# A fused attention and feed-forward kernel: where the block sums of a weight matrix are formed

## The chip, the cores and the metric

The kernel runs on one core of a Trainium2 chip. The metric is device time in microseconds (us) of one execution; the kernel before took 1820.25 us (median of 3 runs, 1819.62 to 1823.83). A core has five engines with instruction queues of their own: PE (TensorE, the matmuls; PEld is its weight load), DVE (VectorE), ACT (ScalarE), POOL (GpSimd) and SP (SyncE, which here only issues DMAs). They meet through semaphores. Sixteen DMA engines move data.

## The reference

Eight batches of 224 tokens of width 512 attend to 750 context rows each (8 heads of 64), and then every token passes through all eight experts of a feed-forward layer:

```
x = x + tanh(g_xattn) * (softmax(q k^T / 8) v @ Wo + bo),  q = layernorm(x) @ Wq, k = ctx @ Wk, v = ctx @ Wv
h = gelu(layernorm(x) @ w1[e] + b1[e])          e = 0..7, 512 -> 1024
y = sum over e of (h @ w2[e] + b2[e])           1024 -> 512
x = x + tanh(g_ffn) * y * norm_gate(x)
```

All inputs are float32. The kernel reaches that precision by splitting each operand into a rounded high part and a low part and adding three products.

## The kernel before

**Stages.** A head, then the attention of batch 0, of batches 1 to 6 (a hardware loop) and of batch 7, then 64 feed-forward steps: two halves of the tokens (896 each), 8 experts, 4 steps of 256 hidden units each. In the attention the order of work on PE, ACT, DVE and POOL is written out in tables (BODY_PLAN, END_PLAN): a word such as `M3.1` is one item of work, `<` means an item of the batch before and `>` one of the batch after. Each engine works its own row off in order; SP's order is the code of its block. PSUM has a ring of four banks, and an item that takes a bank waits until DVE has emptied the bank's last item.

**Items that matter here.** S are scores, R the reciprocal of the softmax row sum, M the scaling of a tile of probabilities (POOL scales the tile of the second query half, L1391), T their transposes on PE (L706), P the product with the values, D the sum of a pair of heads (the split attT, on POOL for odd heads, L1400 and L1402), C the split of the context (L1430, L1433), L and A the layer norms, H the seven products of the very first feed-forward step, which are interleaved into batch 7, W and G the preparation of weights and inputs for them.

**The feed-forward step.** `h = x @ w1` is formed by a scheme with seven block products in place of eight (P1 to P7 in `product`, L754). Its weights are the blocks L11, L12, L21, L22 of the step's part of w1 and sums of them. For each step SP loads four blocks (512 KB, `load_w1`, L497) into `w1_stage`. POOL forms four further blocks from them in `w1_part` (L1487, L1488, L1495, L1501) and splits seven blocks into high and low parts (L1493, L1498 for three, L1504, L1507 for four); then the w2 block (L1518, L1521). It may start to write the split weights of a step once the products of two steps before are done, and the next load of w1 waits for the splits. DVE adds the seven products to the four blocks of h (`h_sums`, L1051), ACT applies gelu, and `second` multiplies with w2 (L781) one step later.

**SP in a middle batch** loads the context of the next batch, stores and reloads x, stores yT, and loads the next batch's rows `xa` (L456) for the layer norm whose first instruction on DVE is L886. In batch 7 it loads the inputs of the feed-forward stage and the first w1 blocks (`load_first`).

Of the kernel before, what the change touches and what calls it, by code (L numbers as in the profile page):

```python
# [5 lines left out]
ALU = mybir.AluOpType  # L6
# [5 lines left out]
P = 128  # L12
# [22 lines left out]
GATE_STEPS = 16  # L35
X_MIXED = ["P7", "P5", "P6", "P4"]
# [51 lines left out]
def plan(text):  # L88

    items = []  # L90
    for word in text.split():
# [22 lines left out]

BODY_PLAN = {
# [22 lines left out]
        D<7 M1.1 L<1.0 L<1.1 M2.1 D1 M3.1 C>0.0 C>0.1 L>0.0 L>0.1 M4.1 D3 M5.1 C>1.0 C>1.1 M6.1 D5 M7.1 M>0.1  # L138
# [25 lines left out]
        D<7 M1.1 L<1.0 L<1.1 Z F M2.1 D1 M3.1 W0.0 G0 G1 G2 W0.1 W0.2 D3 W0.3 G3 W0.4 D5 W1.0 D7 W1.1 W1.2 W1.3  # L164
# [41 lines left out]
def flamingo_kernel(nc, x, ctx, g_xattn, g_ffn, Wq, Wk, Wv, Wo, bo, gate_w, gate_b, rms_w, w1, b1, w2, b2, out,  # L206
                    x2_scratch, xt_scratch):
# [11 lines left out]
    with ExitStack() as st:  # L219
# [117 lines left out]
        b1_loaded, b2_loaded = sem("b1_loaded"), sem("b2_loaded")  # L337
        small_loaded, small_set = sem("small_loaded"), sem("small_set")
# [96 lines left out]
        def _(sp):  # L435
# [43 lines left out]

            load_w(0)  # L480
# [45 lines left out]
            def load_first():  # L526
# [5 lines left out]
                sp.wait_ge(in_psum["S"], number(("S", 0, G - 1, 1), B - 1))  # L532
                load_w1((0, 0, 0))
                sp.dma_start(b1T[:, :], b1).then_inc(b1_loaded, 16)

            def batch(name, plan, b):
# [25 lines left out]
                if name != "last":  # L562
                    load_ctx(b + 1, 1)

# [54 lines left out]
        def _(pe):  # L619
# [16 lines left out]
            def make(item, b, bank_table):  # L636
                kind = item[0]
                if kind in "RMDLAWGUZCNF":
                    return
# [233 lines left out]
        def _(dve):  # L873
# [160 lines left out]
            def h_sums(g, name):  # L1034

                product, other, q, after = {"U2": ("P6", 4, 3, None), "C11": ("P2", 4, 0, None),
                                            "U3": ("P7", 3, 2, None), "C22": ("P5", 2, 1, "U3"),
                                            "V": ("P5", 3, 3, "U3"), "C21": ("P4", 2, 2, "C22"),
                                            "C12": ("P3", 3, 3, "V")}[name]
# [9 lines left out]
                if name == "U2":  # L1049
                    dve.wait_ge(p1_out, upto(1, g, 1))  # L1050
                dve.tensor_tensor(h_sum[:, q, :], product_bank(g, product)[:, 0:TH], h_sum[:, other, :],  # L1051
                                  ALU.add).then_inc(sum_out, 1)
# [317 lines left out]
        def _(pool):  # L1370
# [13 lines left out]
            def handle(item, b):  # L1384
# [8 lines left out]
                elif kind == "D" and item[2] % 2:  # L1393
# [10 lines left out]
                    if pair == 1:  # L1404
                        bias_x(b)
                elif kind == "G":
# [44 lines left out]

            def bias_x(b):
# [22 lines left out]
            def w1_part(g, k):  # L1475
# [4 lines left out]
                def after(n):  # L1480
                    pool.wait_ge(w1_step, upto(6, g, n))
                    alone(pool, passed["pool"])

                if k == 0:
                    pool.wait_ge(w1_loaded, upto(16, g, 16))
                    alone(pool, passed["pool"])
                    pool.tensor_tensor(raw[:, 4], raw[:, 0], raw[:, 3], ALU.add).then_inc(w1_step, 1)  # L1487
                    pool.tensor_tensor(raw[:, 6], raw[:, 1], raw[:, 0], ALU.subtract).then_inc(w1_step, 1)  # L1488
                elif k == 1:
                    if not early(g, 2):  # L1490
                        pool.wait_ge(mix_psum, upto(NM, g, -NM))
                        alone(pool, passed["pool"])
                    pool.tensor_copy(w[:, 0, 0:3], raw[:, 1:4]).then_inc(w1_step, 1)  # L1493
                    after(1)
                    pool.tensor_tensor(raw[:, 5], raw[:, 4], raw[:, 1], ALU.subtract).then_inc(w1_step, 1)  # L1495
                elif k == 2:
                    after(3)
                    pool.tensor_tensor(w[:, 1, 0:3], raw[:, 1:4], w[:, 0, 0:3].bitcast(F32),  # L1498
                                       ALU.subtract).then_inc(w1_split, 1)
                    after(4)  # L1500
                    pool.tensor_tensor(raw[:, 7], raw[:, 2], raw[:, 5], ALU.subtract).then_inc(w1_step, 1)  # L1501
                elif k == 3:
                    after(5)
# [108 lines left out]
```

## Time and profile before

| | |
|---|---|
| median of 3 runs | 1820.25 us |
| profiled execution: span from first to last instruction | 1816.1 us |
| what the median holds beyond that span | 4.15 us |
| PE busy | 1794.9 us, 99% of the span |
| DVE, POOL, ACT busy | 1330.5, 1184.1, 810.9 us |
| granted TensorE clock, mean of the span | 1.000 of full speed |
| DMA traffic | 110.35 MB, 61 GB/s |

The profiled execution has a span and no time of its own apart from it; so the sums are made against the span, and the 4.15 us are taken to stay. Busy time counts neither waits nor DMA issues. "Idle before" in a row is the idle time of that engine just before the instruction, and the name behind the arrow is what ended it. Where an engine is busy all the time and another one is not, only what delays the busy one shows in the end.

### The profile page before, as it was taken

What the parts mean: (1) busy time and instruction counts of PE and PEld (TensorE: products, weight loads), DVE (VectorE), ACT (ScalarE), POOL (GpSimd) and SP (SyncE); (2) the same over time, 40 slices, a digit from 0 to 9 for tenths busy, and PEclk for the clock granted to TensorE, in tenths of its full rate; (3) what the DMA queues carried; (4) which work ended last, traced back from release to release, by engine and by line L of the source; (5) the groups of instructions that cost most, each with busy time, mean ns of one, the idle gap of its engine ahead of it and who ended that gap; (6) DMA issues with size and microseconds to landing.
All of it is one profiled execution on the core that took longest, in us unless ns stands there. A gap on an engine that the chain in (4) does not pass through costs nothing.

```text
span 1816.1 us, 31801 instructions
## 1 busy us (share of the span) xinstructions
PE 1794.9 (99%) x9720; PEld 1615.8 (89%) x9720; DVE 1330.5 (73%) x2308; ACT 810.9 (45%) x1574; POOL 1184.1 (65%) x900
## 2 busy tenths in 40 slices
PE   7999999999999999999999999999999999999999
PEld 7999999999999878888888888888888888888887
DVE  7888878888888877666666766588766767676657
ACT  6767677677766832323232323243232323232322
POOL 5525445263544679777777777699877777777743
PEclk9999999999999999999999999999999999999999
DMA  5111202021120222111111111123412121212111
GB/s 176 39 41 36 57 22 61 21 62 40 34 69 16 92 97 74 66 54 62 58 58 58 58 58 58 47 66 106 127 57 63 52 69 47 69 46 69 46 47 53
DMA packets 52057, 110.35 MB, mean 61 GB/s; under 512 B 13208, under 2 KB 25496, under 8 KB 52000
## 3 DMA queue, kind: packets, MB, share of 16 engines
q1 hardware_dynamic: 52000, 109.64, 19.3%
q8 instruction: 30, 0.49, 0.1%
q14 instruction: 27, 0.22, 0.0%
HBM read 98.61 MB, written 11.01 MB: 60 GB/s over the span
## 4 chain that ended last, share of the span: by engine, by line
PE 96%; DVE 1%; issue 1%; ACT 1%; DMA 0%; SPq 0%; POOL 0%; ACTq 0%; DVEq 0%
PE bank L781 33%; PE scores L754 28%; PE bank L625 19%; PE scores L696 5%; PE bank L706 4%; PE bank L718 4%; PE bank L632 1%; PE scores L839 0%; DVE h_sum L1051 0%; DMA ctx_raw<-in_ctx 0%; ACT hs L1318 0%; PE bank L754 0%; ACT probs L1190 0%; DVE xs L900 0%; ACT h_full L1317 0%
## 5 line engine op out<-in xcount | busy, mean ns | idle before, releaser
L781 PE MATMUL bank<-w2s,hs 128*128 128x512 f32 x2688 | 620.9, 389 | 1.3 <-DVE xres L1018 1.0
L781 PEld LDWEIGHTS bank<-w2s,hs 128*128 128x128 f32 x2688 | 504.4, 188 | 105.1 <-issue 1.5
L754 PE MATMUL scores<-xs,w1s 128*128 128x448 f32 x2646 | 549.5, 366 | 3.6 <-DVE h_sum L1051 3.5
L754 PEld LDWEIGHTS scores<-xs,w1s 128*128 128x128 f32 x2646 | 495.8, 188 | 48.7 <-DVE h_sum L1051 3.8
L1051 DVE TENSOR_TENSOR h_sum<-scores,h_sum 128x448 f32<-128x448 f32 x441 | 262.7, 619 | 183.3 <-PE scores L754 182.8
L1317 ACT ACTIVATE h_full<-h_sum,b1T 128x448 f32<-128x448 f32 x256 | 170.9, 668 | 303.1 <-DVE h_sum L1051 292.4
L1066 DVE TENSOR_TENSOR acc<-bank,acc 128x512 f32<-128x512 f32 x337 | 229.1, 686 | 71.5 <-PE bank L781 62.9
L900 DVE TENSOR_TENSOR hs<-h_full,hs 128x448 fp32r<-128x448 f32 x256 | 237.9, 930 | 52.2 <-ACT hs L1318 52.1
L1190 ACT ACTIVATE h_sum<-scores 128x448 f32<-128x448 f32 x63 | 34.3, 545 | 475.4 <-PE scores L754 475.4
L1391 POOL TENSOR_SCALAR probs<-probs,row_inv 112x750 f32<-112x750 f32 x60 | 130.6, 2176 | 100.1 <-DVE row_inv L989 100.1
L1493 POOL CAST w1s<-w_stage 128x768 fp32r<-128x768 f32 x64 | 69.0, 1078 | 168.5 <-PE scores L754 168.5
L1318 ACT ACTIVATE hs<-h_sum,b1T 128x448 fp32r<-128x448 f32 x256 | 167.7, 655 | 0.0
L1521 POOL TENSOR_TENSOR w2s<-w_stage,w2s 128x1024 fp32r<-128x1024 f32 x64 | 155.1, 2423 | 11.5 <-POOL w2s L1518 11.5
L1507 POOL TENSOR_TENSOR w1s<-w_stage,w1s 128x1024 fp32r<-128x1024 f32 x64 | 155.0, 2422 | 11.3 <-POOL w1s L1504 11.3
L625 PE MATMUL bank<-ctxT,wk 128*128 128x376 f32 (+1 forms) x768 | 147.0, 341 | 8.0 <-DVE ctxT L900 8.0
L625 PE MATMUL bank<-wv,ctxT 128*125 128x256 f32 x1152 | 152.1, 283 | 0.0
L625 PEld LDWEIGHTS bank<-wv,ctxT 128*125 128x125 f32 x1152 | 142.6, 186 | 1.0
L625 PEld LDWEIGHTS bank<-ctxT,wk 128*128 128x128 f32 x768 | 131.5, 191 | 10.4 <-issue 9.4
L1498 POOL TENSOR_TENSOR w1s<-w_stage,w1s 128x768 fp32r<-128x768 f32 x64 | 137.8, 2153 | 0.0
L1234 ACT ACTIVATE probs<-scores,neg_max 112x750 f32<-112x750 f32 x128 | 113.3, 886 | 32.1 <-DVE neg_max L983 20.8
L900 DVE TENSOR_TENSOR probsT<-bank,probsT 125x448 fp32r<-125x448 f32 x192 | 115.9, 618 | 12.7 <-ACT probsT L1190 11.1
L1190 ACT ACTIVATE probsT<-bank 125x448 fp32r<-125x448 f32 x192 | 100.0, 542 | 49.3 <-PE bank L706 49.0
(128 smaller groups left out, 2197.3 us busy)
## 6 DMA issues: line engine op xcount, KB each, us to landing
w_stage<-in_L_ffn_w SPq DMA_DIRECT2D x128, 512.0 KB, 3.5
ctx_raw<-in_ctx SPq DMA_DIRECT2D x16, 376.0 KB, 3.2
ctx_raw<-in_ctx SPq DMA_DIRECT2D x14, 374.0 KB, 3.2
xa<-in_x SPq DMA_DIRECT2D x16, 224.0 KB, 2.7
xres<-in_x SPq DMA_DIRECT2D x16, 224.0 KB, 2.7
x_scratch<-xres SPq DMA_DIRECT2D x16, 224.0 KB, 2.3
xt_scratch<-yT SPq DMA_DIRECT2D x16, 224.0 KB, 2.8
x_raw<-xt_scratch SPq DMA_DIRECT2D x4, 896.0 KB, 7.7
```

The source lines that it names most:

```text
L625: mm = pe.matmul(bank, s[i], m[j], start=first and n == 0, stop=last and n == total - 1)
L754: mm = pe.matmul(product_bank(g, name)[:, 0:TH], w1s[j % 2][:, s, W_OF[name], kc, :], xs[:, i, m, kc, :], start=n == 0, stop=n == 5)
L781: mm = pe.matmul(bank[:, :], hs[j % 2][:, s, ht, t * P:(t + 1) * P], w2s[j % 2][:, m, ht, :], start=n == 0, stop=n == 5)
L900: return dve.tensor_tensor(out, a_, b_.bitcast(F32), ALU.subtract)
L1051: dve.tensor_tensor(h_sum[:, q, :], product_bank(g, product)[:, 0:TH], h_sum[:, other, :], ALU.add).then_inc(sum_out, 1)
L1066: dve.tensor_tensor(home, ps[(3 * j + t) % RING][:, :], b2_sum[:, :] if first else home, ALU.add).then_inc(y_added, 1)
L1190: return act.activation(dst, src, ACT.Copy, scale=scale)
L1317: act.activation(h_full[:, q, :], src, ACT.Gelu, bias=bias)
L1318: act.activation(hs[j % 2][:, 0, ht, half * TH:(half + 1) * TH], src, ACT.Gelu, bias=bias).then_inc(h_act, 1)
L1498: pool.tensor_tensor(w[:, 1, 0:3], raw[:, 1:4], w[:, 0, 0:3].bitcast(F32), ALU.subtract).then_inc(w1_split, 1)
L1507: pool.tensor_tensor(w[:, 1, 3:7], raw[:, 4:8], w[:, 0, 3:7].bitcast(F32), ALU.subtract).then_inc(w1_split, 1)
L1521: pool.tensor_tensor(w[:, 1], w2_stage[:, :, :], w[:, 0].bitcast(F32), ALU.subtract).then_inc(w2_split, 1)
```

## The change

The four sums per step are no longer formed by POOL in the feed-forward stage. The w1 input is laid out anew in DRAM (one array per block, padded to 7 units of 80 rows of 2048 floats). During the attention, seven times:

- SP copies four blocks of one unit from the input to a DRAM scratch `w1_sums` (`copy_blocks`, at the end of batches 0 to 6), 655,360 bytes each.
- One batch later POOL issues seven accumulating DMAs (destination += source, DRAM to DRAM, 655,360 bytes each) in three phases, items `E<0`, `E<1`, `E<2`: four DMAs, then two, then one. Phase 0 waits for the copies, phase 1 for the four DMAs of phase 0, phase 2 for the two of phase 1.

The sums in scratch have the sign that an accumulation gives, so some products come out negative; `h_sums` subtracts where it added before. A step's load is now two DMAs of rows of 1 KB: three blocks from the input and four from scratch, 896 KB instead of 512 KB. In batch 7 SP waits for all 49 accumulating DMAs before the first of these loads.

```diff
 BODY_PLAN pool:
-        D<7 M1.1 L<1.0 L<1.1 M2.1 D1 M3.1 C>0.0 C>0.1 L>0.0 L>0.1 M4.1 D3 M5.1 ...
+        D<7 E<0 M1.1 L<1.0 L<1.1 M2.1 E<1 D1 M3.1 C>0.0 C>0.1 L>0.0 L>0.1 E<2 M4.1 D3 M5.1 ...
 END_PLAN pool:
-        D<7 M1.1 L<1.0 L<1.1 Z F M2.1 D1 M3.1 W0.0 G0 G1 G2 W0.1 W0.2 D3 ...
+        D<7 E<0 M1.1 L<1.0 L<1.1 Z F E<1 M2.1 D1 M3.1 E<2 W0.0 G0 G1 G2 W0.1 W0.2 D3 ...
+            def copy_blocks(u):
+                for k, block in enumerate(("L22", "L11", "L11", "L12")):
+                    sp.dma_start(unit_of(w1_sums, k, u), unit_of(w1, W1_BLOCKS.index(block), u)
+                                 ).then_inc(blocks_copied, 16)
 load_w1:
-                sp.dma_start(w1_stage[:, 0:4], w1[e, j]).then_inc(w1_loaded, 16)
+                sp.dma_start(w1_stage[:, 0:3], step_of(w1, 1, 4, e, j)).then_inc(w1_loaded, 16)
+                sp.dma_start(w1_stage[:, 3:7], step_of(w1_sums, 0, 4, e, j)).then_inc(w1_loaded, 16)
 load_first:
+                sp.wait_ge(blocks_added, 112 * UNITS)
                 load_w1((0, 0, 0))
 SP, end of batches 0 to 6:
                     load_ctx(b + 1, 1)
+                    copy_blocks(b)
 h_sums:
+                if op == "less product":
+                    dve.tensor_tensor(h_sum[:, q, :], kept, new, ALU.subtract).then_inc(sum_out, 1)
+                else:
+                    dve.tensor_tensor(h_sum[:, q, :], new, kept,
+                                      ALU.add if op == "sum" else ALU.subtract).then_inc(sum_out, 1)
+            def add_blocks(u, phase):
+                if phase == 0:
+                    pool.wait_ge(blocks_copied, u * 64 + 64)
+                    terms = [(k, "L21") for k in range(4)]
+                elif phase == 1:
+                    pool.wait_ge(blocks_added, u * 112 + 64)
+                    terms = [(1, "L22"), (3, "L22")]
+                else:
+                    pool.wait_ge(blocks_added, u * 112 + 96)
+                    terms = [(3, "L11")]
+                alone(pool, passed["pool"])
+                for k, block in terms:
+                    pool.dma_start(unit_of(w1_sums, k, u), unit_of(w1, W1_BLOCKS.index(block), u),
+                                   accum_op=ALU.add, max_dma_last_dim=8192).then_inc(blocks_added, 16)
 w1_part (the four tensor_tensor of raw[:, 4] to raw[:, 7] go; what is left):
+                    pool.tensor_copy(w[:, 0, 0:3], raw[:, 0:3]).then_inc(w1_step, 1)
+                    pool.tensor_tensor(w[:, 1, 0:3], raw[:, 0:3], w[:, 0, 0:3].bitcast(F32),
+                                       ALU.subtract).then_inc(w1_split, 1)
+                    pool.tensor_copy(w[:, 0, 3:7], raw[:, 3:7]).then_inc(w1_step, 1)
+                    pool.tensor_tensor(w[:, 1, 3:7], raw[:, 3:7], w[:, 0, 3:7].bitcast(F32),
+                                       ALU.subtract).then_inc(w1_split, 1)
```

POOL in a middle batch, before, from the scaling M1.1 (first row) over the layer norm's two small instructions to M2.1 and the split attT of the pair D1:

```order
L1391 TENSOR_SCALAR probs<-probs,row_inv 112x750 [waits inv_out]
L1380 REGISTER_ALU
L1381 TENSOR_TENSOR rstd<-rstd,minus_half 112x1 [waits ln_var]
L1380 REGISTER_ALU
L1381 TENSOR_TENSOR rstd<-rstd,minus_half 112x1 [waits ln_var]
L1389 REGISTER_ALU
L1391 TENSOR_SCALAR probs<-probs,row_inv 112x750 [waits inv_out]
L1396 ISA
L1398 REGISTER_ALU [waits P_lo_out]
L1400 CAST attT<-att_sum 128x224 [waits O_in_psum]
```

The same place after the change (the scaling is now L1424, attT L1433; w_sums is the scratch, and the first row is one of four alike):

```order
L1500 DMA w_sums<-in_L_ffn_w 80x2048
L1422 ISA
L1424 TENSOR_SCALAR probs<-probs,row_inv 112x750 [waits inv_out]
L1413 REGISTER_ALU
L1414 TENSOR_TENSOR rstd<-rstd,minus_half 112x1 [waits ln_var]
L1413 REGISTER_ALU
L1414 TENSOR_TENSOR rstd<-rstd,minus_half 112x1 [waits ln_var]
L1422 REGISTER_ALU
L1424 TENSOR_SCALAR probs<-probs,row_inv 112x750 [waits inv_out]
L1493 ISA
L1500 DMA w_sums<-in_L_ffn_w 80x2048 [waits blocks_added]
L1500 DMA w_sums<-in_L_ffn_w 80x2048
```

Four DMAs now stand ahead of M1.1, and behind M2.1 a wait for the four with two more DMAs ahead of D1.

POOL in batch 7, before, from M3.1 (first row) through the first weight blocks:

```order
L1391 TENSOR_SCALAR probs<-probs,row_inv 112x750 [waits inv_out]
L1487 TENSOR_TENSOR w_stage<-w_stage 128x256 [waits w1_loaded]
L1488 TENSOR_TENSOR w_stage<-w_stage 128x256
L1473 TENSOR_TENSOR x_mix<-x_raw 128x896 [waits S_in_psum,x_raw_loaded]
L1473 TENSOR_TENSOR x_raw<-x_raw 128x2x448 [waits x_mixed,S_in_psum,x_raw_loaded]
L1473 TENSOR_TENSOR x_mix<-x_raw 128x896 [waits x_mixed,S_in_psum,x_raw_loaded]
L1493 CAST w1s<-w_stage 128x768 [waits P_in_psum]
L1495 TENSOR_TENSOR w_stage<-w_stage 128x256 [waits w1_step]
L1498 TENSOR_TENSOR w1s<-w_stage,w1s 128x768 [waits w1_step]
L1501 TENSOR_TENSOR w_stage<-w_stage 128x256 [waits w1_step]
```

The same place after the change:

```order
L1424 TENSOR_SCALAR probs<-probs,row_inv 112x750 [waits inv_out]
L1500 DMA w_sums<-in_L_ffn_w 80x2048 [waits blocks_added]
L1524 TENSOR_TENSOR x_mix<-x_raw 128x896 [waits S_in_psum,x_raw_loaded]
L1524 TENSOR_TENSOR x_raw<-x_raw 128x2x448 [waits x_mixed,S_in_psum,x_raw_loaded]
L1524 TENSOR_TENSOR x_mix<-x_raw 128x896 [waits x_mixed,S_in_psum,x_raw_loaded]
L1536 CAST w1s<-w_stage 128x768 [waits P_in_psum,w1_loaded]
L1540 TENSOR_TENSOR w1s<-w_stage,w1s 128x768 [waits w1_step]
```

The four sums are gone, the last accumulating DMA stands ahead of the inputs' sums, and the wait for the loaded weights has moved to the first rounding.

SP in batch 7 after the change, at the first loads of the feed-forward stage (x_raw are its inputs, w_stage the weights, h_full here takes b2):

```order
L533 DMA x_raw<-xt_scratch 128x2x896
L520 DMA w_stage<-in_L_ffn_w 128x3x256 [waits blocks_added,S_in_psum]
L521 DMA w_stage<-w_sums 128x4x256
L559 DMA b1T<-in_L_ffn_b 128x64
L486 DMA xt_scratch<-yT 512x1x112 [waits Y_lo_out]
```

Before there was one w_stage load here, and it waited for S_in_psum alone.

## Rows read from the trace of the kernel before

**Rows 1.** The page, part 1: busy time, share of span, instructions.

```profile
PE 1794.9 (99%) x9720; PEld 1615.8 (89%) x9720; DVE 1330.5 (73%) x2308; ACT 810.9 (45%) x1574; POOL 1184.1 (65%) x900
```

**Rows 2.** Stretches: length, then busy time of each engine, clock, DMA share, GB/s.

```profile
256.00:334.00 78.00, 77.94 (x539) 74.89 (x538) 64.02 (x137) 54.69 (x121) 36.28 (x30) 1.00 0.16 43
567.00:650.00 83.00, 78.86 (x480) 69.89 (x479) 70.45 (x137) 62.19 (x122) 49.77 (x41) 1.00 0.19 62
...
1260.00:1800.00 540.00, 540.00 (x2519) 471.47 (x2518) 368.01 (x558) 164.37 (x274) 387.76 (x286) 1.00 0.20 63
```

**Rows 3.** PE's waits, whole run: us in total, times, longest.

```profile
PE bank L625 <- DVE ctxT L900: 8.0, 1, 8.0
PE scores L754 <- DVE h_sum L1051: 3.5, 6, 0.9
```

**Rows 4.** The chain that ended last, two feed-forward pieces: start, us, what.

```profile
1283.52 9.54 PE bank L781 x42
1293.05 8.51 PE scores L754 x42
```

**Rows 5.** Instructions on tile w_stage: count, ns min/median/max.

```profile
L1501 POOL TENSOR_TENSOR w_stage<-w_stage x64: 731/1120/1592, 617.2 to 1775.9; 128x256 f32<-128x256 f32 x64
```

**Rows 6.** POOL in one feed-forward step: start, us, instruction [idle before].

```profile
1283.69 0.83 POOL L1493 CAST w1s<-w_stage 128x768 fp32r<-128x768 f32 x1 [2.33 <-PE scores L754]
...
1290.59 2.40 POOL L1507 TENSOR_TENSOR w1s<-w_stage,w1s 128x1024 fp32r<-128x1024 f32 x1 [0.18 <-POOL w1s L1504]
```

**Rows 7.** The page, part 3: DMA queue, packets, MB, share of 16 engines' span.

```profile
q1 hardware_dynamic: 52000, 109.64, 19.3%
```

**Rows 8.** The page, part 6: DMA issues, count, KB each, us to landing.

```profile
w_stage<-in_L_ffn_w SPq DMA_DIRECT2D x128, 512.0 KB, 3.5
...
xa<-in_x SPq DMA_DIRECT2D x16, 224.0 KB, 2.7
```

**Rows 9.** POOL in the middle batch from 263 us: M1.1, M2.1, D1, M3.1, M4.1.

```profile
265.06 2.17 POOL L1391 TENSOR_SCALAR probs<-probs,row_inv 112x750 f32<-112x750 f32 x1
...
284.57 2.17 POOL L1391 TENSOR_SCALAR probs<-probs,row_inv 112x750 f32<-112x750 f32 x1
289.05 0.37 POOL L1400 CAST attT<-att_sum 128x224 fp32r<-128x224 f32 x1 [2.30 <-DVE att_sum L1010]
...
291.42 2.17 POOL L1391 TENSOR_SCALAR probs<-probs,row_inv 112x750 f32<-112x750 f32 x1 [1.25 <-DVE row_inv L989]
...
302.32 2.18 POOL L1391 TENSOR_SCALAR probs<-probs,row_inv 112x750 f32<-112x750 f32 x1
```

**Rows 10.** PE in the same batch: the transposes T1 and T3.

```profile
273.43 1.02 PE L706 MATMUL bank<-ident,probs 112*125 112x112 f32 x8
...
297.50 0.59 PE L706 MATMUL bank<-ident,probs 112*125 112x112 f32 x4
```

**Rows 11.** SP in the same batch: the load of the next rows xa.

```profile
287.68 0.33 SPq L456 DMA_DIRECT2D xa<-in_x  x1
```

**Rows 12.** DVE in the same batch: a layer norm applied, and the next one's statistics.

```profile
284.77 0.96 DVE L896 TENSOR_SCALAR xa<-xres,mean_var,rstd 112x512 f32<-112x512 f32 x1
...
293.93 0.69 DVE L886 BATCH_NORM_STATS2 stats<-xa 112x6 f32<-112x512 f32 x1
```

**Rows 13.** POOL in batch 7: end of the pair D<7, M2.1, M3.1, first rounding of w1.

```profile
575.96 0.67 POOL L1402 TENSOR_TENSOR attT<-att_sum,attT 128x224 fp32r<-128x224 f32 x1
...
593.59 2.29 POOL L1391 TENSOR_SCALAR probs<-probs,row_inv 112x750 f32<-112x750 f32 x1 [1.95 <-DVE row_inv L989]
...
601.75 2.17 POOL L1391 TENSOR_SCALAR probs<-probs,row_inv 112x750 f32<-112x750 f32 x1 [0.99 <-DVE row_inv L989]
...
613.94 0.83 POOL L1493 CAST w1s<-w_stage 128x768 fp32r<-128x768 f32 x1
```

**Rows 14.** PE in batch 7: the transposes T2, and the first product H0.

```profile
598.17 1.02 PE L706 MATMUL bank<-ident,probs 112*125 112x112 f32 x8
...
628.95 1.45 PE L754 MATMUL bank<-xs,w1s 128*128 128x448 f32 x6 [0.40 <-DVE b_sum L944]
```

More of the change, by code:

```diff
@@ L35 @@
 GATE_STEPS = 16
+UNITS = B - 1
+UNIT = 5
+UNIT_ROWS = UNIT * P * 2 * P // 2048
 X_MIXED = ["P7", "P5", "P6", "P4"]
@@ L112, with unit_of, step_of @@
 }
+W1_BLOCKS = ("L21", "L11", "L12", "L22")
+def unit_of(t, k, u):
+    return t[k, bass.ds(u * UNIT_ROWS, UNIT_ROWS), :]
+def step_of(t, k0, k1, e, j):
+    rows = P * 2 * P // 2048
+    at = t[k0:k1, bass.ds(e * (JS * rows) + j * rows, rows), :]
+    return at.rearrange("k r (p n) -> (r p) k n", n=2 * P)
 BODY_PLAN = {
@@ L1034, in h_sums @@
             def h_sums(g, name):
[L1036 to L1039, printed above, removed]
+                product, other, q, after, op = {"U2": ("P6", 4, 3, None, "product less"),
+                                                "C11": ("P2", 4, 0, None, "sum"),
+                                                "U3": ("P7", 3, 2, None, "less product"),
+                                                "C22": ("P5", 2, 1, "U3", "sum"),
+                                                "V": ("P5", 3, 3, "U3", "sum"),
+                                                "C21": ("P4", 2, 2, "C22", "sum"),
+                                                "C12": ("P3", 3, 3, "V", "product less")}[name]
                 dve.wait_ge(mix_psum, upto(NM, g, MIX.index(product) + 1))
@@ L1050, in h_sums @@
                     dve.wait_ge(p1_out, upto(1, g, 1))
-                dve.tensor_tensor(h_sum[:, q, :], product_bank(g, product)[:, 0:TH], h_sum[:, other, :],
-                                  ALU.add).then_inc(sum_out, 1)
+                new, kept = product_bank(g, product)[:, 0:TH], h_sum[:, other, :]
+                if op == "less product":
[3 more added lines that the diff above has]
+                                      ALU.add if op == "sum" else ALU.subtract).then_inc(sum_out, 1)
             def h_low(g, q):
@@ L1478, in w1_part @@
                 raw, w = w1_stage, w1s[j % 2]
[L1480 to L1489, printed above, removed]
+                if k == 1:
+                    pool.wait_ge(w1_loaded, upto(32, g, 32))
@@ L1490, in w1_part @@
                     if not early(g, 2):
                         pool.wait_ge(mix_psum, upto(NM, g, -NM))
[L1492 to L1495, printed above, removed]
+                    alone(pool, passed["pool"])
+                    pool.tensor_copy(w[:, 0, 0:3], raw[:, 0:3]).then_inc(w1_step, 1)
@@ L1496, in w1_part @@
                 elif k == 2:
-                    after(3)
-                    pool.tensor_tensor(w[:, 1, 0:3], raw[:, 1:4], w[:, 0, 0:3].bitcast(F32),
+                    pool.wait_ge(w1_step, upto(2, g, 1))
+                    alone(pool, passed["pool"])
+                    pool.tensor_tensor(w[:, 1, 0:3], raw[:, 0:3], w[:, 0, 0:3].bitcast(F32),
                                        ALU.subtract).then_inc(w1_split, 1)
-                    after(4)
-                    pool.tensor_tensor(raw[:, 7], raw[:, 2], raw[:, 5], ALU.subtract).then_inc(w1_step, 1)
```

23 lines of the change are left out of this document (13 added, 10 removed).

## The prediction

> **What bounds the kernel now.** I read the busy shares first. PE is busy for 1794.9 us, 99% of the span, every other engine for 73% or less [rows 1]. Then the stretches, because an average can hide a stage with another limit. In a middle batch of the attention PE works 77.94 of 78.00 us, in the second half of the feed-forward stage 540.00 of 540.00, at the full clock; only the passage between the two stages has a gap, 78.86 of 83.00 [rows 2]. Third, what PE waits for: 8.0 us once in the head, for the split context, and 3.5 us in six pieces for `h_sum` [rows 3]; no row names POOL or a weight. Fourth, the chain that ended last: in the feed-forward stage it is 9.54 us of second products and 8.51 us of first products in turn, all PE, 18.05 us a step [rows 4]. So time can be won only in PE's gaps, and is lost wherever something new comes later than PE wants it.
>
> **The change, part by part.** *POOL's sums go.* Four instructions a step, between 0.73 and 1.12 us each [rows 5], in 64 steps: 187 to 287 us of POOL. In the steady steps this is worth nothing: POOL's first rounding of w1 already waits 2.33 us for PE [rows 6], and its result is used more than a whole step later. *The signs* change one operand order and an ALU code of DVE instructions whose number and size stay: 0.
>
> *Loads of a step.* First a rate: the queue moved 109.64 MB in 19.3% of 16 engines' span [rows 7], so while busy it moves 109.64 MB / (0.193 x 1816.1 us) = 313 KB per us. A 512 KB (524 thousand bytes) load lands in 3.5 us [rows 8]; 524/313 = 1.7 of these are data and 1.8 fixed. The xa load (229 thousand bytes in 2 KB rows, 2.7 us [rows 8]) gives 254 KB per us by the same fixed part. The new 917 thousand bytes take 4.7 us by the first rate, and 9.0 at half the second, which is my bound for rows of 1 KB. What hides it: POOL's work from the first rounding to the last split of w1 now takes 1283.69 to 1292.99, 9.3 us [rows 6], less two sums of 1.1 then 7.1; from there to the next rounding, one step of 18.05 after the first, remain 11.0 us. Hidden at either end. Cost 0.
>
> *Copies on SP.* Four issues at 0.33 us [rows 11], behind the batch's last loads. Queued behind them is the next batch's context load, which waits for POOL's split in any case. Their data, 2.6 MB, has most of a batch before POOL asks for it. Cost 0.
>
> *POOL's DMA issues.* The trace has no DMA on POOL. From below: 0.33 us, SP's issue [rows 11]; from above: 2.17 us, POOL's longest instruction here [rows 9]. I take 1.0, nearer to SP's row, since an issue works on no tile. Four stand ahead of M1.1. In the middle batch M1.1 runs 265.06 to 267.23 [rows 9], and PE wants it at 273.43 [rows 10]: 6.2 us of slack against 4.0, so 0; a loss begins at 1.55 us an issue, and at 2.17 it is 2.5 us a batch, 15 in six. Two more stand behind M2.1, which ends at 286.74, ahead of D1 (289.05) and M3.1 (291.42, 2.17 long) [rows 9], which T3 wants at 297.50 [rows 10]. With D1's 1.1 us they may start as late as 294.2, so the wait in phase 1 may last until 292.2. Phase 2 precedes M4.1 (302.32), with still more room.
>
> *How long four accumulating DMAs take.* No such DMA is in the trace. Each has 655 thousand bytes to read twice (the sum and the block) and to write once. If the passes overlap fully, one pass counts: 2.1 us each at 313 KB per us, four in 10.2 us with 1.8 fixed. If all three come one after another: 6.3 each, four in 26.9. I take the two reads, with the write beside them, since loads, one-sided reads, are what the row of the rate mostly holds: 4.2 each, four in 18.6, two in 10.2, one in 6.0. In a middle batch they start near 266 and have landed at 285, before the wait at 286.74: 0. Phase 1's two, from 289 on, land at 299, before 302: 0.
>
> One rule of the Trainium skill speaks for less: page "Collectives: The Full Stack", section "The bandwidth ceiling: the fold count and why AG ≠ RS ≠ AR", says that a reducing transfer runs at about half a copy's rate, because each chunk has two source reads on one ring, and measures 32.35 against 62.28 GB/s on two DMA engines. No run here shows it yet; by that (16 GB/s per engine) an estimate is 2.6 us a DMA and 12 us for four, and the sum would be 0.
>
> *Batch 7 is the tight one.* The pair D<7 ends at 576.63 [rows 13]; the four DMAs are issued from there, start at 577.6 and land at 596.2. Phase 1 stands ahead of M2.1, which ran at 593.59 [rows 13]. Two issues later, at 598.2, M2.1 starts, ends at 600.5, and T2, which PE ran at 598.17 [rows 14], is 2.3 us late. Phase 1's two land at 607.4; M3.1, 2.3 later than its 601.75, is done at 606.2; phase 2 goes out at 608.4 and lands at 614.4. Only then does SP load the first w1 blocks (behind it wait b1, a store of yT and the next loads, all with more room), which land 4.7 to 5.4 us later, near 619.5. Their rounding ran at 613.94 [rows 13], 616.2 with the shift: 3.3 late. Two sums of at least 0.73 and 1.12 us behind it are gone, some 2 us, so H0, at 628.95 before [rows 14], is late by 2.3 and 1.0: 3.3 us.
>
> *A second rule, on starved descriptors.* The row: DVE's only operation here with SBUF on both sides and one tensor read, the layer norm, runs 0.96 us from 284.77 [rows 12], and phase 1's DMAs are issued after 286.74, so it costs 0; on top of one it would cost at most 0.96 us, 7 in seven batches. The Trainium skill, page "SBUF — State Buffer", section "SBUF: two separate sides", says that a DMA issued by GpSimd cannot write its descriptors while VectorE holds the shared port in a two-port mode. By that rule the sum stays as it is, unless the DMAs slide under such an instruction.
>
> **The sum.** 0 in the head, 0 in the middle batches, +3.3 in batch 7, 0 in the feed-forward steps: 1816.1 + 3.3 of span, and with the 4.15 us by which the median exceeds the span, 1823.5 us. That is within 0.3% (5.5 us, about what a measurement can tell from no change), 1814.8 to 1825.7.
>
> **The rivals.**
>
> *Slower: the accumulations become the bound of the attention's end.* One mechanism: POOL's in-order queue waits for DMAs, and the scalings behind it reach PE late. It decides from 16 us for four in batch 7 (593.4 less 577.6, where T2 begins to slip) and from 26 us in a middle batch (292.2). At the upper end, 26.9 us: the four land at 604.5, M2.1 ends at 608.8, PE is 10.6 late; phase 1's two (14.4 us) land at 619.9, phase 2's one (8.1 us) at 629, the load at 634, against 624.5 with the shift, less the 2 us saved: H0 18 late. In the middle batches 0.7 each, 4 in six. Sum +22: 1842 us. For it: the row rates are those of plain loads, and loads in both directions share 16 engines with the DMAs. Against: the DMA share in these stretches is 0.16 to 0.19 [rows 2], so little competes.
>
> *Slower: the issues, or the xa load.* At 2.17 us an issue the loss is 15 us, as above, and in batch 7 some 3 more. Or phase 1's two DMAs, at 287 to 298, share the engines with the xa load, issued at 287.68 [rows 11] and due at 293.93 [rows 12]: it lands at 290.4, 3.5 us early, and if it takes twice as long, still in time; if three times, DVE stops for 1.9 us, and PE for as much, since its four banks are emptied by DVE. That is 11 in six. Time: 1829 to 1841.
>
> *Faster.* If the POOL time that is freed lets DVE and ACT run earlier in the passage, PE could win there: 4.1 us of idle in 567 to 650 [rows 2] and the 3.5 us behind h_sum [rows 3], 7.6 at the very most, 1812.6; the pieces are waits for DVE, not for POOL, so hardly any of it is to be had. More than 5.5 us would need most of it.
>
> *The change does not do what it says*, that is, POOL keeps its 187 us: excluded, since the instructions are gone; but their going being worth nothing is my forecast.
>
> **How the numbers follow.** Forecast, between 0 and +5: chance 0.54. Slow accumulation: 0.25. Slow issues or xa: 0.16. Faster: 0.05, of which 0.04 by over 0.3%. Slower by over 0.3% is nearly all of the two rivals and a little of the forecast's upper end, 0.42; the rest, 0.54, is no change. The range for 8 in 10 goes from 1817, a few us won in the passage, to 1842, the end of the three-pass bound; the forecast's own is 1820 to 1825.5.
>
> **What would show it.** In the changed profile: POOL busy down by about 200 us and PE's 9.54 and 8.51 us pieces unchanged; no PE wait in a middle batch; POOL idle ahead of phase 1 in batch 7 for a DMA on w_sums, and T2 and H0 late by 2 to 4 us; POOL's DMA issues near 1 us. Wrong, if PE works less than 77.9 of 78 us in a middle batch, if it waits there for probs or DVE for xa, if a step in the feed-forward stage waits for its load, or if four accumulations take over 20 us or under 15.

## The result, and the profile after

The changed kernel takes 1881.3 us (median of 4 runs, 1881.06 to 1884.47), the kernel before 1820.2 beside it (4 runs): ratio 1.0337, 95% interval 1.0322 to 1.0352. I had forecast 1823.5 and a range up to 1842; it is slower than even the range. All times here and below are medians; one run of e7 that took 4616.0 us is left out of its median as a slow run.

First the busy shares of the changed kernel, which answer to [rows 1]:

```profile
span 1879.9 us, 31674 instructions
...
PE 1818.1 (97%) x9720; PEld 1637.0 (87%) x9720; DVE 1343.8 (71%) x2308; ACT 812.5 (43%) x1574; POOL 1028.1 (55%) x693
```

The span grew from 1816.1 to 1879.9, by 63.8 us. PE is idle for 61.8 us (1879.9 less 1818.1) where it was idle for 21.2, and the same 9720 matrix instructions are busy for 23.2 us more. So two losses are to be explained, some 41 us of new waits and some 23 us of slower work. The stretches say where (columns as in [rows 2]: length, busy time of PE, PEld, DVE, ACT, POOL, granted clock, DMA share, GB/s):

```profile
100.00:180.00 80.00, 77.38 (x535) 74.09 (x534) 64.59 (x135) 54.08 (x119) 42.44 (x37) 1.00 0.54 134
180.00:260.00 80.00, 68.78 (x443) 65.48 (x443) 52.37 (x114) 44.78 (x99) 37.06 (x33) 0.89 0.53 127
260.00:340.00 80.00, 73.83 (x475) 70.55 (x474) 57.95 (x124) 48.55 (x107) 35.22 (x32) 0.94 0.52 127
...
580.00:660.00 80.00, 70.25 (x454) 67.54 (x455) 55.01 (x117) 46.17 (x102) 42.84 (x38) 0.91 0.46 114
...
1320.00:1860.00 540.00, 540.00 (x2520) 471.61 (x2519) 370.42 (x553) 163.19 (x273) 301.40 (x174) 1.00 0.26 84
```

The loss is in the attention. The feed-forward stage is what it was: 540.00 of 540.00 us of PE at the full clock, with POOL at 301 us instead of 388. In the attention PE loses up to 11 us in 80, the granted clock goes down to 0.89, and the DMA engines are busy for about half of the time instead of 0.16. What PE waits for (us in total, times, longest), against [rows 3]:

```profile
PE bank L732 <- POOL probs L1424: 30.2, 7, 9.5
PE bank L732 <- DVE queries L990: 12.0, 4, 3.3
PE bank L651 <- DVE ctxT L926: 8.5, 2, 8.2
PE scores L780 <- DVE h_sum L1084: 2.5, 2, 1.8
```

Two waits are new, and 30.2 + 12.0 = 42.2 us is about the new idle time. The transposes wait for the scaling of the probabilities on POOL, and for a DVE instruction on the queries.

**The first wait: POOL's queue stands still.** POOL and then PE in the second batch, start, us, instruction, idle before:

```profile
190.54 0.67 POOL L1435 TENSOR_TENSOR attT<-att_sum,attT 128x224 fp32r<-128x224 f32 x1
191.35 2.54 POOL L1500 DMA_DIRECT2D w_sums<-in_L_ffn_w  x3
204.60 0.81 POOL L1500 DMA_DIRECT2D w_sums<-in_L_ffn_w  x1 [10.71 <-issue]
205.18 2.46 POOL L1424 TENSOR_SCALAR probs<-probs,row_inv 112x750 f32<-112x750 f32 x1
```

```profile
207.78 1.99 PE L732 MATMUL bank<-ident,probs 112*125 112x112 f32 x8 [8.04 <-POOL probs L1424]
```

Each issue takes 0.8 to 0.9 us. But between the third and the fourth of E0's DMAs POOL does nothing for 10.71 us, and nothing in the profile is named that it waits for. M1.1 behind it comes late, and PE stands for 8.04 us. The DMA rows for the first and the third of the three tell when they landed (they were issued at 191.35 and near 193):

```profile
w_sums<-in_L_ffn_w POOLq DMA_DIRECT2D x1, 640.0 KB, 6.0
```

```profile
w_sums<-in_L_ffn_w POOLq DMA_DIRECT2D x1, 640.0 KB, 11.6
```

The first is there at 197.4, the third at 204.6: POOL goes on when all that it sent out has landed, not when the first has. Such gaps stand ahead of the 6th, 11th, 16th, 31st, 41st and 46th of the 49 accumulating DMAs (5 to 12 us each), every fifth; at the 21st, 26th and 36th, each the first of its phase, nothing was out. The line's total:

```profile
L1500 POOL DMA_DIRECT2D w_sums<-in_L_ffn_w x49: 806/915/1686, 110.9 to 666.5; - x49
its engine sat idle before it (us, times) until:
  issue: 52.5, 13
```

**The slower work.** The clock around this stop, in stretches of 2 us:

```profile
198.00:200.00 2.00, 1.74 (x10) 1.33 (x8) 1.09 (x2) 1.64 (x4) 0.00 (x0) 1.00 1.00 201
200.00:202.00 2.00, 0.00 (x0) 0.00 (x0) 1.67 (x4) 0.53 (x2) 0.00 (x0) 0.91 0.95 208
202.00:204.00 2.00, 0.00 (x0) 0.00 (x0) 0.00 (x0) 0.00 (x0) 0.00 (x0) 0.50 0.77 190
...
208.00:210.00 2.00, 2.00 (x10) 2.00 (x11) 0.45 (x1) 1.03 (x2) 0.00 (x0) 0.50 1.00 209
210.00:212.00 2.00, 2.00 (x8) 2.00 (x7) 1.75 (x6) 0.76 (x2) 0.57 (x1) 0.53 0.01 0
212.00:214.00 2.00, 2.00 (x15) 2.00 (x15) 0.41 (x1) 0.96 (x2) 0.00 (x0) 1.00 0.00 0
```

PE stops near 199.7; the granted clock goes from 1.00 to 0.50 (from 2.4 to 1.2 GHz) and is still there when PE works again, until about 212. Eight transposes take 1.99 us instead of 1.02 [rows 10]. So this stop cost 8 us of idle time and some 2 of half-speed work behind it.

**The second wait: the xa load.** SP, DVE and PE in the third batch, against [rows 11, 12]:

```profile
312.04 0.34 SPq L473 DMA_DIRECT2D xa<-in_x  x1
```

```profile
322.46 0.69 DVE L912 BATCH_NORM_STATS2 stats<-xa 112x6 f32<-112x512 f32 x1 [4.17 <-DMA xa<-in_x]
```

```profile
325.28 1.18 PE L732 MATMUL bank<-ident,probs 112*125 112x112 f32 x4 [3.33 <-DVE queries L990]
```

Phase 1's two DMAs were issued at 310.96. The xa load, started at 312.04 beside them, lands 10 us later; DVE, whose queue is in order, stops for 4.17 us ahead of its statistics, the queries behind them are late, and PE stands for 3.33. Part 6 of the page (count, KB each, median us to landing), against [rows 8]:

```profile
w_sums<-in_L_ffn_w POOLq DMA_DIRECT2D x49, 640.0 KB, 8.5
...
w_sums<-in_L_ffn_w SPq DMA_DIRECT2D x28, 640.0 KB, 8.0
...
xa<-in_x SPq DMA_DIRECT2D x16, 224.0 KB, 8.3
```

### The profile page after: what moved, and what is told of

Same layout as the page of the kernel before. It is cut to its first block, busy times and chain, and to the rows that moved or that the text cites. A ratio compares the mean times of both kernels' runs of the same rounds, so it can differ in the third digit from the quotient of the medians.

```text
span 1879.9 us, 31674 instructions
## 1 busy us (share of the span) xinstructions
PE 1818.1 (97%) x9720; PEld 1637.0 (87%) x9720; DVE 1343.8 (71%) x2308; ACT 812.5 (43%) x1574; POOL 1028.1 (55%) x693
## 3 DMA queue, kind: packets, MB, share of 16 engines
q0 software_dynamic: 4704, 32.12, 9.2%
## 4 chain that ended last, share of the span: by engine, by line
PE 82%; issue 8%; DVE 3%; DMA 2%; POOL 2%; ACT 1%; SPq 0%; POOLq 0%; DVEq 0%; ACTq 0%
PE bank L807 32%; PE scores L780 28%; PE bank L651 11%; PE bank L732 3%; PE scores L722 3%; PE bank L744 2%; DMA xa<-in_x 2%; POOL probs L1424 1%; DVE neg_max L1009 1%; PE bank L780 1%; DVE queries L990 0%; PE bank L658 0%; PE scores L865 0%; POOL w_sums L1500 0%; DVE stats L912 0%
## 5 line engine op out<-in xcount | busy, mean ns | idle before, releaser
L1084 DVE TENSOR_TENSOR h_sum<-scores,h_sum 128x448 f32<-128x448 f32 x378 | 223.8, 619 | 144.8 <-PE scores L780 144.4
L926 DVE TENSOR_TENSOR hs<-h_full,hs 128x448 fp32r<-128x448 f32 x256 | 252.2, 986 | 52.9 <-ACT hs L1351 52.8
L1099 DVE TENSOR_TENSOR acc<-bank,acc 128x512 f32<-128x512 f32 x337 | 225.0, 683 | 59.3 <-PE bank L807 58.0
L1223 ACT ACTIVATE h_sum<-scores 128x448 f32<-128x448 f32 x63 | 34.3, 545 | 479.3 <-PE scores L780 479.3
L1424 POOL TENSOR_SCALAR probs<-probs,row_inv 112x750 f32<-112x750 f32 x60 | 136.2, 2270 | 90.9 <-DVE row_inv L1015 90.7
L1547 POOL TENSOR_TENSOR w1s<-w_stage,w1s 128x1024 fp32r<-128x1024 f32 x64 | 162.9, 2545 | 11.3 <-POOL w1s L1543 11.2
L651 PE MATMUL bank<-ctxT,wk 128*128 128x376 f32 (+1 forms) x768 | 152.5, 349 | 8.5 <-DVE ctxT L926 8.5
L732 PE MATMUL bank<-ident,probs 112*125 112x112 f32 x768 | 111.0, 286 | 42.5 <-POOL probs L1424 30.2
L732 PEld LDWEIGHTS bank<-ident,probs 112*125 112x125 f32 x768 | 106.4, 201 | 49.8 <-issue 34.3
L651 PEld LDWEIGHTS bank<-ctxT,wk 128*128 128x128 f32 x768 | 136.7, 198 | 11.2 <-issue 9.7
```

Source lines behind the costliest of these rows:

```text
L651: mm = pe.matmul(bank, s[i], m[j], start=first and n == 0, stop=last and n == total - 1)
L732: last = pe.transpose(bank[0:KT, at:at + QT], probs[0:QT, (h % 2) * 2 + qt, kt * KT:(kt + 1) * KT], ident[0:QT, 0:QT])
L926: return dve.tensor_tensor(out, a_, b_.bitcast(F32), ALU.subtract)
L1084: dve.tensor_tensor(h_sum[:, q, :], new, kept, ALU.add if op == "sum" else ALU.subtract).then_inc(sum_out, 1)
L1099: dve.tensor_tensor(home, ps[(3 * j + t) % RING][:, :], b2_sum[:, :] if first else home, ALU.add).then_inc(y_added, 1)
L1424: pool.tensor_scalar(probs[0:QT, i, :], probs[0:QT, i, :], row_inv[0:QT, i:i + 1], None, ALU.mult).then_inc(probs_scaled[qt], 1)
```

## The experiments

Theory 1: the space for POOL's descriptors, the entries by which its DMAs are handed to the DMA engines (1024 bytes in this program, a number that was there before the change), holds five of these DMAs, and when it is used up POOL stands until everything out has landed. Theory 2: the accumulating transfers share the engines with loads that the attention waits for, xa above all. Theory 3, the rival: what is lost beside that lies in POOL's issues, the copies, the new loads or the signs.

**Four times the space (e1).**

```diff
-    nc = ... dynamic_dma_scratch_size=1024)
+    nc = ... dynamic_dma_scratch_size=4096)
```

> The only edit: the space for the descriptors of POOL's DMAs is 4096 bytes a partition instead of 1024. Theory 1 (the space holds five of the 49 accumulating DMAs; before every further group POOL's queue stands until the earlier ones have landed, and the M1.1 or M2.1 behind it comes late): a four times longer space has that stop at about every 21st DMA, so at 2 places at most instead of 9; of POOL's 52.5 us of idle time ahead of the accumulating DMAs under 15 us are left, of TensorE's 30.2 us of waits for probs under 8, and a part of the 23 us of slower clock goes with them: 1832 to 1846 us. Theory 2 (the accumulating DMAs are slow and share the transfer engines with the loads that the attention waits for): nothing changes, 1876 to 1886 us. Theory 3 (POOL's issue itself costs more than thought): nothing changes either, and the 0.9 us an issue stays as it is under every theory.

1860.2 us, ratio 1.0210 (1.0176 to 1.0245). One stop is left, ahead of the 24th DMA, in batch 4; the next counted place, the 47th, is the first of a phase 1, with nothing out.

```profile
360.34 1.71 POOL L1500 DMA_DIRECT2D w_sums<-in_L_ffn_w  x2
370.33 1.67 POOL L1500 DMA_DIRECT2D w_sums<-in_L_ffn_w  x2 [8.28 <-issue]
```

```profile
PE bank L732 <- DVE queries L990: 18.7, 6, 3.8
...
PE bank L732 <- POOL probs L1424: 6.0, 2, 5.7
```

POOL's idle time ahead of the line fell from 52.5 to 10.0 us and PE's wait for probs from 30.2 to 6.0, as Theory 1 said. The time is worse than I expected from it, because the other wait grew, from 12.0 us in four batches to 18.7 in six.

**Twice the space (e2).** The same line with 2048.

> The only edit: 2048 bytes instead of 1024. Theory 1: the stop comes about every 10th or 11th DMA, so at 4 places instead of 9, each as long as before (up to 12 us) if at the wrap POOL waits for everything that is out; then about half of the loss by the stops stays, 1845 to 1865 us. Theory 1b (POOL waits only until the entries that it needs are free): a DMA ten places back has long landed, so there is no stop at all and the time is that of 4096 bytes. Theories 2 and 3: 1876 to 1886 us.

1866.2 us, 1.0244 (1.0209 to 1.0279), just above the 1865 that was expected at most. Gaps stand ahead of the 23rd, 34th and 45th DMA, every 11th; the 12th is the first of a phase 1, with nothing out.

```profile
360.69 0.86 POOL L1500 DMA_DIRECT2D w_sums<-in_L_ffn_w  x1 [0.44 <-issue]
366.94 2.50 POOL L1500 DMA_DIRECT2D w_sums<-in_L_ffn_w  x3 [5.38 <-issue]
```

The DMA ten places back had landed long ago, so Theory 1b (only the entries needed must be free) falls; POOL waits for all that is out. Periods of 5, 11 and 23 in 1024, 2048 and 4096 bytes put a DMA between 171 and 178 bytes. Counted in entries of 16 bytes, a size that no run here shows, that is 11 entries a DMA and no other whole number.

**No additions (e3).**

```diff
                 elif kind == "E":
-                    add_blocks(b - 1, item[2])
+                    pass
```

SP's wait ahead of the first w1 load is then for the copies.

> Left out: the 49 accumulating DMAs, so that the block sums are copies of single blocks. The 28 copies by SP, the feed-forward loads from the new tensor and the signs in the sums of products stay. Theories 1 and 2: everything that is lost is lost by the accumulating DMAs, so 1816 to 1826 us, with TensorE's waits for probs at 0 and its busy time in the feed-forward unchanged. Rival (the copies, the new loads or the signs cost something): over 1830 us.

1819.8 us, 0.9990 (0.9977 to 1.0004). The xa load takes 2.7 us again.

```profile
span 1818.2 us, 31474 instructions
...
PE 1800.0 (99%) x9720; PEld 1621.3 (89%) x9720; DVE 1341.7 (74%) x2308; ACT 811.7 (45%) x1574; POOL 985.3 (54%) x644
```

Copies, loads and signs together cost nothing that can be measured, and the 200 us that POOL no longer works (985 against 1184 [rows 1]) bring nothing. Theory 3 is left with the issues alone. (PE's busy time differs by 5.1 us from that of before at nearly the same span, so the changed kernel's slower work is 18.1 us against this run and 23.2 against before, its new idle time 43.6 or 40.6.)

**Copies in the place of additions (e4).**

```diff
-                                   accum_op=ALU.add, max_dma_last_dim=8192).then_inc(blocks_added, 16)
+                                   max_dma_last_dim=8192).then_inc(blocks_added, 16)
```

> The 49 DMAs of POOL copy a block instead of adding it to what stands in the sums (same place, same bytes written, half the bytes read; the sums are then single blocks), with 1024 bytes for descriptors. Theory 1: if a copying DMA takes as many entries as an accumulating one, the stops come at the same places and are as long as what is out needs to land: 1850 to 1880 us; if it takes half, they come at every 10th or 11th, 1830 to 1850 us. Theory 2 (transfer time alone): POOL has no stops, and what is late is late by the transfers: the landings and the xa loads are about half as long, so about half of the loss, 1845 to 1855 us.

1828.8 us, 1.0042 (1.0027 to 1.0057), a little under both guesses. Gaps stand ahead of the 11th, 31st and 41st DMA, every 10th, which is 6 entries of 64 for one:

```profile
187.70 1.80 POOL L1500 DMA_DIRECT2D w_sums<-in_L_ffn_w  x3
195.92 0.52 POOL L1500 DMA_DIRECT2D w_sums<-in_L_ffn_w  x1 [6.42 <-issue]
```

The queue's packets (4704) and bytes are those of the changed kernel, but they took 5.2% of the engines' time in place of 9.2%, and the xa load lands in 6.5 us, not 8.3: DVE waits 5.0 us for it in all, not 17.9, and PE 0.9 us for queries. 11 entries against 6 would be 5 rows an engine with two sources against 5 with one, and one entry more, if the 80 rows are spread evenly over 16 engines. That is how the Trainium skill describes the reducing transfer (page "Collectives: The Full Stack", section "The bandwidth ceiling: the fold count and why AG ≠ RS ≠ AR"): it emits two read descriptors per chunk where a copy emits one. The runs agree; the even spread and the one entry more are my inference.

**A smaller space that fits the batch (e5).** The same line with 1280: 80 entries, seven DMAs of 11, just what a batch issues.

> The only edit: 1280 bytes for the descriptors, less than a third of the 4096 that left two stops. From the stops of the three sizes before (every 5th, 11th and 23rd DMA) one accumulating DMA takes 11 entries of 16 bytes, so 1280 bytes hold seven, just what one batch issues. Theory 1: the stop then falls ahead of the first of E0, when all earlier DMAs landed some 40 us before, so POOL never stands: under 3 us of idle time ahead of the accumulating DMAs except where they wait for one another, no wait of TensorE for probs, and less than with 4096 bytes: 1845 to 1856 us. Rival (the more space the better, whatever the count): between the times of 1024 and 2048 bytes, 1866 to 1881 us.

1852.0 us, 1.0164 (1.0136 to 1.0192): less space than 4096 bytes and a better time, though the two ratios' intervals overlap a little. One stop was left, ahead of the 27th DMA, where the count has none. It stands between phase 1's two DMAs of batch 4, and that is the one batch in which PE did not wait for queries (15.9 us in the five others).

**Phase 1 behind the xa load (e6, e7).**

```diff
-        D<7 E<0 M1.1 L<1.0 L<1.1 M2.1 E<1 D1 M3.1 C>0.0 C>0.1 L>0.0 L>0.1 E<2 M4.1 D3 M5.1 ...
+        D<7 E<0 M1.1 L<1.0 L<1.1 M2.1 D1 M3.1 E<1 C>0.0 C>0.1 L>0.0 L>0.1 M4.1 D3 E<2 M5.1 ...
```

In e6 with 1024 bytes, in e7 with 1280.

> 1024 bytes as in the changed kernel; in the middle batches E<1 stands behind M3.1 instead of behind M2.1 and E<2 behind D3, so that the two DMAs of the second phase start when the xa loads have landed. Theory 2: DVE's waits for xa (17.9 us) and TensorE's for queries (12.0 us) go, the xa load takes 2.7 to 4 us again; the stops stay: 1855 to 1870 us. Rival 3 (what is lost beside the stops is lost by POOL's issues or by the sums' transfers elsewhere): 1876 to 1886 us.

> Both edits: 1280 bytes, and E<1 and E<2 later. Theories 1 and 2 together hold all of the loss: no wait for probs, none for queries, a granted clock near 1 through the attention, 1818 to 1828 us. Rival 3: what neither explains stays, over 1835 us.

e6: 1866.3 us, 1.0248 (1.0220 to 1.0277); e7: 1826.0 us, 1.0026 (1.0011 to 1.0040). Both times are as expected. In e6 the wait for queries is gone and the stops are not:

```profile
PE bank L732 <- POOL probs L1424: 26.7, 5, 9.8
```

In e7 the wait for queries is gone, and all stops but one, 5.15 us ahead of the 27th DMA, in batch 4 as in e5:

```profile
378.05 0.80 POOL L1500 DMA_DIRECT2D w_sums<-in_L_ffn_w  x1 [5.15 <-issue]
```

```profile
384.18 1.69 PE L651 MATMUL bank<-wv,ctxT 128*125 128x256 f32 x12 [1.97 <-POOL ctxT L1468]
```

PE waits there 2.0 us for the split context and 0.9 for probs. The middle batch from 256 us, with the DMA engines as busy as in the changed kernel (0.55) and POOL issuing as much, is that of [rows 2]:

```profile
256.00:334.00 78.00, 77.92 (x539) 74.83 (x538) 63.97 (x137) 54.67 (x122) 42.42 (x37) 1.00 0.55 136
```

```profile
294.20 1.74 POOL L1500 DMA_DIRECT2D w_sums<-in_L_ffn_w  x2
```

```profile
294.61 0.68 DVE L912 BATCH_NORM_STATS2 stats<-xa 112x6 f32<-112x512 f32 x1
```

Phase 1 now goes out when xa is there. The four times side by side (us):

| space | E<1, E<2 in place | E<1, E<2 later |
|---|---|---|
| 1024 bytes | 1881.3 | 1866.3 |
| 1280 bytes | 1852.0 | 1826.0 |

The space is worth 29 and 40 us, the order 15 and 26. Together they give 11 us more than the sum of the two alone. A part of that is that a stop between phase 1's two DMAs keeps the second one off the xa load: in the changed kernel batches 1 and 6 had such a stop and no wait for queries, the four between had the wait (12.0 us); with 1280 bytes five batches have it (15.9). With the slower clock behind it, that is about half of the 11 us; the rest is not explained. Theory 3 has at most the 6 us that e7 lies above before, and the one stop that is left takes some 3 of them.

**A short last unit (e8).** This is e7 with one more edit: in batch 7 the seventh unit is added over the two parts that hold weights, not over five.

```diff
+    rows = UNIT_ROWS
+    if isinstance(u, int) and u == UNITS - 1:
+        rows = (NE * JS - (UNITS - 1) * UNIT) * (UNIT_ROWS // UNIT)
...
```

> As the run before, and the seventh unit, of whose five parts only two hold weights, is added over these two parts alone (the padding is left out, the result is the same). Shorter phases in the last batch, in which the feed-forward's first load waits for the last addition: 0 to 4 us less than the run before, 1817 to 1826 us. If the last batch isn't held up by the additions, no difference.

1824.1 us, 1.0013 (1.0001 to 1.0024), 1.9 less than e7, with intervals that overlap. With the order mended, all stops gone but the one in batch 4 (5.17 us here), and the last batch shortened, this is the best version with additions, and it does not beat the kernel before.

**Other spaces (e9, e10, e12).** e9 is e8 with 3712 bytes, e10 the changed kernel with 1408, e12 e8 with 1408.

> As e8_short_last, with 3712 bytes: 232 entries, 21 DMAs of 11 entries, so the stop falls at the 22nd and the 43rd, each the first of a batch, with everything before it landed. With 1280 bytes one stop of 5 us before the 27th DMA was left that this count doesn't explain (TensorE waited 2.0 us for ctxT there). Theory 1 with the count alone: no stop at all, 1819 to 1824 us. If that stop has another cause than the space (it comes at the 27th DMA whatever the size), it is there again: 1822 to 1826 us. Neither theory lets it be faster than before by more than a measurement shows, since without any addition the time was that of before.

> The changed kernel's order with 1408 bytes: 88 entries, eight DMAs. Theory 1: stops at the 9th, 17th, 25th (second, third and fourth of the four DMAs of E0) and 41st (second of E1); those at the 33rd and 49th are hidden behind a wait that is there anyway. So more space than 1280 bytes and more stops: 18 to 35 us of idle POOL ahead of the accumulating DMAs (9.0 with 1280), 1860 to 1872 us against 1852. Rival (more space is better): 1845 to 1853 us.

> As e8_short_last (E<1 and E<2 later, short last unit), with 1408 bytes, the size that showed no stop at all in the changed kernel's order. If the stops belong to the size and not to the order: no stop, no wait for probs or ctxT, granted clock 1.00, 1819 to 1823 us, between e3_copies_only and e8. If a stop shows up at another place it costs 5 to 11 us there, 1824 to 1833 us. In neither case less than before by over 0.3%.

e9: 1830.5 us, 1.0055 (1.0042 to 1.0069), above both guesses. My count was wrong: there is a stop ahead of the 39th DMA,

```profile
498.50 2.54 POOL L1503 DMA_DIRECT2D w_sums<-in_L_ffn_w  x3
511.53 0.80 POOL L1503 DMA_DIRECT2D w_sums<-in_L_ffn_w  x1 [10.48 <-issue]
```

and PE waits 7.9 us. e10: 1855.2 us, 1.0183 (1.0163 to 1.0203), where I expected stops at the 9th, 17th, 25th and 41st and there is none; the time lies between my two guesses. It has no wait for probs, and 18.9 us of waits for queries in six batches. e12: 1829.6 us, 1.0038 (1.0024 to 1.0052): no stop in six batches, and two in batch 7, whose DMAs are of another size.

```profile
578.35 0.85 POOL L1503 DMA_DIRECT2D w_sums<-in_L_ffn_w  x1
584.11 0.77 POOL L1503 DMA_DIRECT2D w_sums<-in_L_ffn_w  x1 [4.91 <-issue]
588.57 1.56 POOL L1503 DMA_DIRECT2D w_sums<-in_L_ffn_w  x2 [3.69 <-issue]
```

So 11 entries a DMA predicts the stops for the three powers of two, and not for 1280, 1408 and 3712 bytes. Which rule holds there stays open; the gaps end, here too, with the landing of what was out (in e9 the third DMA, issued near 499.9, lands after 11.6 us, at 511.5), and e10, without a gap, had no wait for probs.

**A stop without any transfer (e11).** e3 with a pause of POOL in the place of E<0:

```diff
+                elif kind == "E" and item[2] == 0:
+                    for k in range(16):
+                        pool.wait_ge(paused, (b - 1) * 16 + (k + 1))
+                        alone(pool, passed["pool"])
+                        pool.memset(pause[:, :], 0.0).then_inc(paused, 1)
```

> As e3_copies_only (no additions, no transfer of POOL's), with 16 MEMSETs of 128x512 that wait for one another at E<0 of each batch, 10 to 13 us in which POOL does nothing for the others. It prices a stop of POOL by itself, without any transfer: M1.1 had 6.2 us to spare, so TensorE waits 4 to 7 us for probs in each of seven batches, 28 to 48 us of idle time. If TensorE's stops bring the slower clock by themselves, its busy time grows as well, by 10 to 27 us, and the granted clock shows 0.9 to 0.98 in the 80 us stretches: 1858 to 1890 us. Rival (the slow clock comes with the accumulating transfers): busy time as in e3 (1800 us), clock 1.00, 1846 to 1866 us.

1870.4 us, 1.0274 (1.0253 to 1.0294), within what Theory 1 gave.

```profile
span 1867.3 us, 31795 instructions
...
PE 1814.8 (97%) x9720; PEld 1636.0 (88%) x9720; DVE 1345.6 (72%) x2308; ACT 810.8 (43%) x1574; POOL 1042.7 (56%) x757
```

```profile
PE bank L734 <- POOL probs L1427: 32.2, 7, 5.2
```

```profile
180.00:260.00 80.00, 75.59 (x505) 72.59 (x505) 60.31 (x129) 51.80 (x115) 42.82 (x44) 0.96 0.24 75
```

A pause is 16 times 0.53 us and 0.15 us of waiting between two, 10.8 in all; less the 6.2 of slack it should delay PE by 4.6. It does: seven waits of 4.6 us, and beside them 14.8 us more of busy time than in e3, at a granted clock of 0.96 with the DMA share at 0.24. So the slower clock comes with PE's stops and not with the transfers; e7, with all the transfers, has 1.00 from 20 to 580 us. A stop of 4.6 us costs about 2 us more behind it.

## Why the prediction was wrong

**The step that failed: POOL's DMA issues.** I bounded an issue between 0.33 and 2.17 us from the durations of instructions. The duration was right: 0.9 us against my 1.0. What I did not see is that an issue can be refused for a time by a resource that stands in the program with its size, 1024 bytes, and that before the change no DMA of POOL used; e1, e2 and e5 change this number alone, and the stops move or go. The price is not spread over the issues but falls on every fifth, as long as the transfers out need, up to 11.6 us: beyond the 6.2 us of slack that I had worked out for M1.1, and that the pause of e11 confirms. In time it is 29 us as the kernel stands, 40 with the other loss mended. The Trainium skill, page "DMA: Bandwidth & Descriptors", section "SWDGE vs HWDGE vs iDMA", tells of the place: descriptors of GpSimd's DMAs are appended to rings in a carved-out part of SBUF, the on-chip memory, and those of SP's are not. SP's copies, with the same bytes, show no such stop: four issues took 2.6 to 3.6 us in every batch, more than the 1.3 I had taken.

**The xa load: seen, priced too low, and left to a rival.** I wrote that it is due 3.5 us after it lands and that three times its time would stop DVE for 1.9 us, 11 us in six batches. It took 3.1 times (8.3 us) and 3.7 times in e1 (10.0), DVE stopped for up to 5.0 us (e2), and moving phase 1 away was worth 15 to 26 us. The mechanism stood in the rival, but the sum had it at 0: I had no row for a load beside large transfers, and twice its time alone, which I took for harmless, was too little. The Trainium skill, page "DMA: Bandwidth & Descriptors", section "Queues, rings and completion order", says that each engine serves its queues in turn, a packet at a time; a load between two large additions then waits for theirs at each turn. A load that takes 3 to 4 times as long fits that; the page gives no such factor, and no run here shows the turns themselves.

**The clock: not in the sum at all.** Every rival took "late by x" as "longer by x". Of the 63.8 us, 18 to 23 are added busy time, most of it work at the lower clock behind the stops, 0.4 us and more for each us of idle time (e11: 14.8 to 34.3, against e3). With it my own rival's 11 us would have been some 16.

**Right.** The additions' speed: four in a row land in 17.4 us (batch 4: the first issued at 373.70, the last near 376.5 with 14.6 us to its landing) where I took 18.6, and the first of three in 6.0, my figure for one; phase 2's one, beside SP's copies, took 11.1, where nothing hung on it. That fits two reads beside a write, as assumed. The estimate of 12 us for four from the Trainium skill's rate (page "Collectives: The Full Stack", section "The bandwidth ceiling: the fold count and why AG ≠ RS ≠ AR") was too short. So the rival of slow accumulation falls for the middle batches, where it needed 26 us. The copies, the loads of a step (the second part, issued 0.4 us behind the first, lands in 4.3: 4.7 together, my lower bound), the signs and the worthlessness of POOL's freed time: together 0, by e3. "Faster" was rightly given little: without any addition the ratio is 0.9990 (0.9977 to 1.0004). The rule on starved descriptors was not tested; no run isolates it.

**The last batch: the path was right, the size too large.** In e7, without a stop there, the four land after 18.1 us, past the 16 from which the rival decides, and POOL waits for them ahead of phase 1, as forecast:

```profile
598.90 1.75 POOL L1500 DMA_DIRECT2D w_sums<-in_L_ffn_w  x2 [3.08 <-DMA w_sums<-in_L_ffn_w]
```

```profile
603.03 1.10 PE L732 MATMUL bank<-ident,probs 112*125 112x112 f32 x8 [0.52 <-POOL probs L1424]
```

But T2 is only 0.5 us late, not 2.3. Counted from the end of D<7, H0 starts 2.4 us later than before (at 635.49), and 1.1 of these stand in e3 too, so the additions cost some 1.3 us there against +3.3. (My sum also had a slip: 3.3 less some 2 is 1.3, not 1.0.) That e8's 1.9 us come from this batch is not shown: its H0, at 635.64, is no earlier.

**The chances.** Slower had 0.42, but the range ended at 1842. Both things that made it slower were outside the two mechanisms' ends, since the queue's block had no bound at all and the clock no price.

## What to carry to other kernels

When an engine gets its first DMAs, ask not only what an issue takes but what it can be blocked by: how many may be out, and what stands behind the blocked issue in that engine's queue. A wait in an in-order queue is to be compared with the slack of the next instruction behind it, and the stop of a full PE is to be priced at more than its length, here at 1.4 times. Put large transfers where no small load is due, even if the engines look idle on average.

## What the hardware showed that I had not expected

POOL, when its descriptor space is used up, waits until all of its DMAs have landed, even where the first of them had landed 7.2 us earlier (197.4 against 204.6). A space of 1280 bytes was no worse than one of 4096 (1852.0 against 1860.2 us): each had one stop of POOL to be seen, with 1280 bytes between phase 1's two DMAs, with 4096 ahead of M1.1. Where the space runs out for sizes that are no power of two is open. And two accumulating DMAs of 640 KB between DRAM tensors make a 224 KB load beside them 3 to 4 times as long (2.7 to 8.3 and 10.0 us), two copying ones 2.4 times (6.5 us).
